# ScalarE's copies and activations for TensorE ahead of its ends of rows, in a graph network kernel with passes cut into steps

## What is computed

```
def _L0(x, src, dst, w, w_self, w_neigh):                    # pass 0
    out = x @ w_self.T + segment_sum(w[:, None] * x[src], dst) @ w_neigh.T
    return out / max(sqrt(sum(out * out, axis=1)), 1e-12)

def _gin_layer(h, src, dst, W1, b1, W2, b2, eps, gamma, beta):   # passes 1, 2, 3
    z = (1.0 + eps) * h + segment_sum(h[src], dst)
    m = relu(z @ W1 + b1) @ W2 + b2
    return relu(layer_norm(m + h, gamma, beta))

x = _layernorm(x + _L0(x, ...))
x = _layernorm(x + three _gin_layer(x, ...))
x = _layernorm(x + _L2(x, ...))      # pass 4, then a mixture of experts and a batch norm
x = _layernorm(x + _L3(x, ...))      # pass 5
```

## Time and profile before

| what | value |
|---|---|
| median of three executions | 6144.3 us |
| the profiled execution, its own time | 6154.02 us |
| its span, first to last instruction | 6152.4 us |
| PE busy, share of the span | 5039.2 us, 82% |
| PEld busy | 4187.6 us, 68% |
| DVE busy | 3758.3 us, 61% |
| ACT busy | 1678.2 us, 27% |
| POOL busy | 3744.4 us, 61% |
| mean granted clock of TensorE | 0.917 of full speed |

### The profile page before, as it was taken

How to read it: one execution, slowest core, us unless ns; L and a number is a source line. 1 busy time by engine, 2 the same in 40 slices (tenths; PEclk the granted TensorE clock), 3 DMA queues, 4 the chain that set the end, 5 groups by cost and what they waited for, 6 DMA issues and landing times.

```text
span 6152.4 us, 104768 instructions
## 1 busy us (share of the span) xinstructions
PE 5039.2 (82%) x36004; PEld 4187.6 (68%) x36004; DVE 3758.3 (61%) x13502; ACT 1678.2 (27%) x4718; POOL 3744.4 (61%) x3737
## 2 busy tenths in 40 slices
PE   5878886699997999878888799950599986788887
PEld 3767675478775888757777688840588863577665
DVE  5676777377875899658787322242477756454543
ACT  3777776111111111112222100000233322233332
POOL 6766767677776777766666677743200023777776
PEclk8999998799998999989999899975799987899998
DMA  5443434677778888976666777751799962333333
GB/s 152 130 129 122 132 123 135 206 224 225 223 222 264 273 272 270 289 234 201 195 199 210 241 221 220 220 158 49 239 307 319 323 215 79 112 112 112 112 113 97
DMA packets 702174, 1180.93 MB, mean 192 GB/s; under 512 B 131306, under 2 KB 510312, under 8 KB 698924
## 3 DMA queue, kind: packets, MB, share of 16 engines
q0 software_dynamic: 212192, 625.22, 34.9%
q1 hardware_dynamic: 489450, 548.94, 27.4%
HBM read 1010.58 MB, written 164.46 MB: 191 GB/s over the span
## 4 chain that ended last, share of the span: by engine, by line
PE 37%; POOL 20%; DVE 13%; issue 13%; DMA 10%; ACT 5%; SPq 2%; DVEq 0%; ACTq 0%; POOLq 0%
POOL ring L2245 13%; PE PS L2340 12%; PE PS L2316 6%; POOL more L2245 5%; PE PS L2458 3%; PE PS L2319 3%; DMA ring<-expert_inputs 3%; PE PS L2402 2%; PE PS L2546 2%; PE PS L2555 2%; DMA pick<-dense_blocks 2%; PE PS L2362 2%; POOL expert_inputs L2260 2%; PE PS L2443 1%; ACT HH L2733 1%
## 5 line engine op out<-in xcount | busy, mean ns | idle before, releaser
L2245 POOL DMA_INDIRECT ring<-planes,REC x1566 | 1563.1, 998 | 650.0 <-issue 495.9
L2340 PE MATMUL PS<-HH,pick 128*128 128x256 bf16 (+1 forms) x7836 | 988.8, 276 | 82.5 <-DMA pick<-dense_blocks 47.4
L2340 PEld LDWEIGHTS PS<-HH,pick 128*128 128x128 bf16 x7836 | 767.3, 99 | 208.0 <-DMA pick<-dense_blocks 54.8
L2245 POOL DMA_INDIRECT ring<-in_x,REC x555 | 597.3, 1076 | 271.8 <-issue 147.2
L2319 PE MATMUL PS<-ring,pick 128*128 128x256 f32 x2160 | 629.1, 419 | 156.5 <-DMA ring<-table,REC 105.8
L2316 PE MATMUL PS<-ring,pick 128*128 128x256 bf16 (+1 forms) x4698 | 628.2, 276 | 71.1 <-DMA ring<-planes,REC 69.5
L2245 POOL DMA_INDIRECT ring<-table,REC x525 | 504.3, 961 | 261.6 <-issue 256.7
L2245 POOL DMA_INDIRECT more<-planes,REC x522 | 522.4, 1001 | 180.6 <-issue 149.9
L2319 PEld LDWEIGHTS PS<-ring,pick 128*128 128x128 f32 x2160 | 411.6, 204 | 305.8 <-DMA ring<-table,REC 139.4
L2316 PEld LDWEIGHTS PS<-ring,pick 128*128 128x128 bf16 x4698 | 451.3, 98 | 165.3 <-DMA ring<-planes,REC 89.1
L2340 PE MATMUL PS<-HH,ring 128*128 128x256 bf16 (+1 forms) x3924 | 513.5, 276 | 56.1 <-DMA ring<-dense_blocks 36.0
(11 more groups left out here) (362 smaller groups left out, 9163.6 us busy)
## 6 DMA issues: line engine op xcount, KB each, us to landing
HH<-in_L_gnn_w SPq DMA_DIRECT2D x280, 512.0 KB, 5.1
pick<-dense_blocks SPq DMA_DIRECT2D x480, 160.0 KB
ring<-dense_blocks SPq DMA_DIRECT2D x240, 160.0 KB
HH<-planes SPq DMA_DIRECT2D x64, 576.0 KB, 7.2
dense_blocks<-HH SPq DMA_DIRECT2D x20, 1568.0 KB, 6.1
planes<-pick SPq DMA_DIRECT2D x147, 192.0 KB
ring<-planes,REC POOLq DMA_INDIRECT x1566
expert_inputs<-VEC SPq DMA_DIRECT2D x41, 512.0 KB
```

Source lines behind the costliest of these rows:

```text
L2245: pool.indirect_dma_start(slot_row(k, slot, 0, RP if dense else D), None, planes[k] if dense else tables[k], bass.IndirectOffsetOnAxis(ap= ...
L2340: last = mm(bank(5 + n % 2, w), block, plane(m, t, w), start=t == 0 and m == 0, stop=t == NT - 1 and m == 2, skip_group_check=True)
```

## The change

In ACT's list the events of a step are walked twice: first Z, T, H and GT of all tiles in it, then F, R and M. No other engine's list is changed.

```
@@ -2788,14 +2788,15 @@
                             copy_transposes(k, p)
                         if name == "H":
                             hidden(k, p)
+                        if name == "GT":
+                            gate_copy(p)
+                    for name, p in events(k, g):
                         if name == "F" and k != 4:
                             finish(k, p)
                         if name == "R":
                             high_part(k, p)
                         if name == "M":
                             middle_part(k, p)
-                        if name == "GT":
-                            gate_copy(p)
                     for b, n in bin_step(k, g):
```

## The result

The changed kernel takes 6235.6 us, the median of five executions (6221.1 to 6238.5), against 6144.9 us before (five, 6137.9 to 6165.9). The ratio is 1.0132, with a 95% interval from 1.0111 to 1.0152: slower, as forecast, by about 81 us by the ratio where 46 were forecast (the two medians are 91 us apart). 6235.6 lies 8 us beyond the range that ended at 6228, while the ratio on the median of 6144.3 us before the change puts it at 6225. The profiled execution took 6229.57 us with a span of 6227.9 us, 75.5 us longer than before.

What follows compares the result with a forecast made beforehand. PE was taken to have little slack beside DVE, above all in pass 2, so late DVE work delays PE. Passes 0 to 3 summed as -3 + 20 + 44 - 15 = +46 us on 6144.3: 6190 us, range 6130 to 6228.

Steps and rivals of the forecast that it cites:

- What bounds the kernel, and where the waits would go: PE's 98 us of waits for ACT's copies (69.8 in pass 3, 28.5 in pass 0) go, but other gaps follow.
- Pass 2, +44: Late DVE one-hots stall PE's histogram at 35 places, 1.25 us each: +44 us, ends 25 and 60.
- root hold: Passes 1 to 3: root stands behind the TZT copy, which waits for PE's transposes; DVE waits, 2.0 us at one place.
- rounding hold: Passes 1 to 3: rounding stands behind the relu, which waits for PE's W1 product; DVE 4.1 us late at one place.
- Pass 1, +20: About half of 30 binning hand-offs from DVE to PE stall by 1.3 us each: +20 us, ends 0 and 39.
- rival D: Much slower, 6251 us, 12%: SP's late row stores hold back dense loads, and pass 2's clock falls to 0.96.
- Pass 3, -15: TZT waits go, PE waits for DVE instead; DVE's 50.2 us of waits bound the gain, 40 holds take 36: -15 us.
- Pass 0, -3: TZ waits before the transposes mostly move to ACT's one-hots behind them: -3 us, ends -28.5 and +8.
- B: Faster, 6097 us, 10%: pass 3 gives back all 70 us of TZT waits; pass 2 loses only 25.
- C: No change, 6144 us, 28%: pass 3 gives 35, pass 0 gives 3, pass 1 costs 8, pass 2 costs 30.
- A: The forecast itself, 50%: DVE's holds cost more than the removed waits give; 6190 us, range 6176 to 6215.

Runs made afterwards that it cites:

- roots_held: Kernel before, but in passes 1 to 3 only T (copy to TZT) goes ahead on ACT, H staying behind R: ratio 1.0050, 31 us slower.
- pass2_only: Kernel before with ACT's new order in pass 2 alone: ratio 1.0098, 60 us slower.
- pass1_late_store: Kernel before with ACT's new order in pass 1 alone and SP storing finished rows of pass 1 one step later: ratio 0.9997.
- between_roots: Kernel before, but in pass 3 the copy to TZT stands between the two roots of the preceding tile's finish: ratio 0.9939, median 6113.8 us.
- rounding_held: Kernel before, but in passes 1 to 3 only H (the relu) goes ahead on ACT, T staying behind F: ratio 1.0117, 72 us slower.
- pass3_only: Kernel before with ACT's new order in pass 3 alone: ratio 0.9995, no change.

## Why the prediction was right in its direction and short in its size

**What bounds the kernel, and where the waits would go.** Right. The 98 us of waits vanished to 1 us, and the kernel got slower. In pass 0 the next wait took over within the same step, as in the earlier trace rows.

**Pass 2, +44, measured +60.** The mechanism was right: a new group of 40.9 us in 63 waits, where "some 40 us in 40 to 70 waits" had been written. Even its size was: the +44 priced the stalls, and the waits for the tables grew by 39 us. The split between the holds was wrong, without harm to the sum, and that was luck: I read one place and gave the root hold 1.05 us and the rounding hold 0.65 us. On the chip the rounding hold alone costs 45 us and the root hold 27. The place shown begins with DVE early; a DVE that stays late after a rounding hold meets no root hold, but it meets the next rounding hold all the same, because that one waits for an event at the end of the following step. I wrote the first half of that sentence and not the second. (DVE waited 17 times for the root and 41 times for the rounding, and 38 times for the root in roots_held.)

What made the term short is that 41 us of waits made the pass 60 us longer: I had priced a stall at its wait. PE's idle time grew by 42 us and its busy time by 18 us. In pass2_only it grew by 13.1 us at an unchanged clock of 0.97, while the busy times of its six lines, each taken alone, grew by 3.3 us together. The other 9.8 us are then overlap between matmuls of neighbouring lines, lost around each of 64 stalls, some 0.15 us each. The clock can be ruled out inside the pass. Between the same two instructions, some 2400 matmuls apart, in the kernel before, in roots_held and in pass2_only:

```profile
2007.20:2262.80 255.60, 245.49 (x2405) 215.89 (x2404) 228.42 (x1196) 35.06 (x112) 189.49 (x198) 1.00 0.88 274
2014.00:2277.20 263.20, 247.17 (x2404) 215.03 (x2402) 224.39 (x1194) 34.68 (x112) 188.11 (x197) 1.00 0.84 264
2009.50:2288.90 279.40, 250.52 (x2405) 213.44 (x2404) 229.90 (x1204) 35.64 (x112) 186.38 (x196) 1.00 0.82 249
```

The histogram stalls 1, 15 and 28 times there, the granted clock is 1.00 in all three, and PE is busy 245.5, 247.2 and 250.5 us: up to 0.19 us more for each stall. That it is overlap which is lost is a reading of the busy times; no run tested it by itself.

**Pass 1, +20, measured +18 in the changed kernel and +22 alone.** The size was right by luck and the step was wrong. It said that half of 30 binning hand-offs stall. Waits of that size came (20 us in 13 waits in pass1_late_store), and the pass is no longer for them, since the waits for gathers shrink instead. The loss went with rival D's mechanism: SP stood at late rows with the dense loads behind, and with the store moved it is gone. "The loads have three buffers" was the argument against it, and PE waited 12 times for them in pass 1 before, 46.5 us, and 26 times after, 81.7 us. D was priced together with a fall of the clock in pass 2 from 1.00 to 0.96; over the whole pass it fell from 0.97 to 0.96 and inside it (1990 to 2250 us) it stayed at 1.00, so that half of D did not come.

**Pass 3, -15, measured -4.** The step was right in that other waits for DVE took the place of the 70 us, and in that the holds eat most of a gain which stays under 50 us. between_roots, without holds, gains 36 us; the holds cost 33 of these 36, where I had taken 36 of 50. I had charged them all to the root. By roots_held, which gains 11, the root hold costs 25 of the 33, and the rounding hold 8 on top of it (24 where it stands alone, in rounding_held).

**Pass 0, -3, measured +7 in the changed kernel and -1 to +12 alone.** The mechanism was right: of the 28 us of waits that went, 24 came back at the one-hots. The +7 lies inside the bounds that were given, and whether the pass got longer at all is not settled.

**Rivals.** B needed pass 3 to give over 60 us; pass3_only gives 9 at the most. C needed passes 1 and 2 to lose 38 us together; they lose 78 in the changed kernel. Between A and D, the outcome lies with the mechanism of A in pass 2 and the part of D's that concerns SP in pass 1.

**The strategy rule.** The forecast had set the Trainium skill's page "Perfetto Trace Analysis", section "Optimization Strategy" (find the gaps, see what ends them, let it start sooner), against another gap right behind. The runs show both sides: the same dependency made to start sooner gave -38 us where it was put into ACT's idle time, 11 us off the pass where the copy alone was put ahead of the finish (roots_held), and 0 where the relu was moved with it (pass3_only). The rule holds for what starts sooner, and says nothing of what the mover then stands in front of.

## What to carry to other kernels

When an instruction is moved forward on an in-order engine, ask what it waits for and not only who waits for it: a copy that stands at the end of another engine's step turns everything behind it into work of that step's end. Put it into a gap in which the engine waits anyway (between two roots here), and both sides gain. And follow lateness into every queue, the queue of the engine that issues loads above all: a store that waits for a late row holds back the loads behind it, and moving that store by one step took the whole measurable loss of pass 1 away.

## What the runs showed of the hardware that was not expected

- A stall of PE cost more than its wait. 64 stalls with 41.6 us of waits made a pass 57 us longer with the same matmuls at the same mean granted clock of 0.97. The waits for the tables grew by 40.1 us, the other waits by 4 and the busy time by 13.1 us. Where the granted clock was 1.00 throughout, each stall came with up to 0.19 us more of busy time.
- With less idle time PE's own work was shorter too. In pass 3 of between_roots PE is busy 649.2 us at a granted clock of 0.94, against 664.3 us at 0.91 before (2622 to 3421 us), with the same matmuls: 15 of the 36 us gained are there. 10 of these 15 are in the W1 product (L2443, 66.8 to 56.9 us), which stood right behind the waits for TZT. The clock is a mean over the two levels of 1.2 and 2.4 GHz. It is not the waits for TZT as such: after the change they are gone as well, but PE's idle time is 132 us as it was (135 us before, 114 in between_roots), the clock is 0.91, and PE is busy 663 us.
- Building the tables of pass 2 ahead of the events cost 14 us with no hold at all. DVE then waited 51.2 us for PE's histograms to free the tables, and pass 2 was 8 us longer, 2 us beyond the longest that was seen where it is untouched. Why the whole kernel lost 0.23% by it is not explained further.
